# The first of sixteen rows: slot maxima ahead of the next row's statistics on VectorE, the second projection inside the expert product, one zero product moved

## The reference

```
xn  = layernorm(x)
out = x + attention(xn) + experts(xn)

attention: q,k,v = xn @ Wqkv + bqkv, 16 heads of 8; q and k normalised to length 1;
           feat = exp(clip(q_hat @ omega * sqrt(2 s) - s, -20, 20)) * const    (2 x 32 features)
           causal linear attention: ctx = (feat_q . feat_k, masked) @ v / denominator; @ Wout + bout
experts:   xn2 = rms_norm(xn) * gamma_x;  se = rms_norm(slot_embeds) * gamma_slot   (512 slots)
           logits = xn2 @ se.T                       (256 tokens x 512 slots)
           slots = softmax over tokens(logits).T @ xn2
           processed = gelu(slots @ w1) @ w2
           y = softmax over slots(logits) @ processed
```

## Time and profile before

| what | us |
|---|---|
| median of 3 runs | 448.09 |
| lowest, highest | 447.37, 450.14 |
| the profiled execution: its time | 448.38 |
| the profiled execution: its span | 446.6 |
| TensorE busy in the span | 434.6 (97%) |
| VectorE, ScalarE, GpSimd busy | 348.6, 320.1, 186.4 |

### The profile page before, as it was taken

The page is one execution under the profiler, slowest core; times in us unless marked ns, Lnnn a source line. Parts: engine busy times, 40 slices in busy tenths (PEclk is TensorE's granted clock), DMA queues, the critical chain, the costliest instruction groups (busy, mean ns, idle before and its releaser), DMA issues.

```text
span 446.6 us, 15786 instructions
## 1 busy us (share of the span) xinstructions
PE 434.6 (97%) x5726; PEld 363.9 (81%) x5726; DVE 348.6 (78%) x872; ACT 320.1 (72%) x533; POOL 186.4 (42%) x278
## 2 busy tenths in 40 slices
PE   6889999999999999999999999999999999999896
PEld 3578888898888889888888888888888888888785
DVE  7968796978778697877969787797978779676553
ACT  4648686867858687695868779586877858677681
POOL 5405564344345434444543444454344445434320
PEclk9889999999999999999999999999999999999999
DMA  4400302030200203020020302002020200303001
GB/s 93 105 25 2 61 12 52 14 60 16 47 26 9 50 12 59 12 47 24 5 54 12 58 12 47 24 2 57 12 57 14 47 12 1 60 1 61 2 1 25
DMA packets 45323, 14.37 MB, mean 32 GB/s; under 512 B 35376, under 2 KB 45168, under 8 KB 45296
## 3 DMA queue, kind: packets, MB, share of 16 engines
q1 hardware_dynamic: 44448, 13.48, 14.7%
q10 hardware_dynamic: 720, 0.53, 0.4%
q0 software_dynamic: 128, 0.01, 0.1%
HBM read 3.44 MB, written 2.10 MB: 12 GB/s over the span
## 4 chain that ended last, share of the span: by engine, by line
PE 93%; DVE 3%; ACT 2%; issue 1%; DVEq 0%; ACTq 0%
PE x L1070 19%; PE p_s L1120 10%; PE p_t L1120 8%; PE x L1238 8%; PE x L1271 7%; PE x L1280 6%; PE x L1292 6%; PE x L1133 5%; PE p_s L1133 5%; PE x L1211 3%; PE p_s L1105 2%; PE x L1222 2%; PE x L1246 2%; PE x L1187 2%; PE p_t L1105 1%; PE x L1230 1%
## 5 line engine op out<-in xcount | busy, mean ns | idle before, releaser
L488 POOL TENSOR_TENSOR s_sb<-s_sb,causal 128x256 f32<-128x256 f32 x96 | 68.4, 733 | 79.4 <-ACT s_sb L584 79.4
L578 ACT ACTIVATE feat<-arg,f_bias 128x1024 f32<-128x1024 f32 x64 | 71.7, 1147 | 8.4 <-DVE arg L848 8.3
L848 DVE TENSOR_SCALAR arg<-p_s,f_low,f_high 128x1024 f32<-128x1024 f32 x32 | 42.9, 1339 | 19.6 <-PE p_s L1105 13.1
L1120 PEld LDWEIGHTS p_s<-feat 64*64 64x64 f32 x1024 | 38.8, 132 | 17.1 <-issue 15.5
L329 POOL TENSOR_TENSOR qk_sq<-qkv 128x512 f32<-128x512 f32 x15 | 15.6, 1040 | 85.9 <-DVE qkv L825 85.9
L1120 PE MATMUL p_s<-feat 64*64 64x256 f32 (+3 forms) x1024 | 49.5, 309 | 1.3 <-ACT feat L578 1.3
L482 POOL TENSOR_TENSOR s_sb<-s_sb,causal 128x512 f32<-128x512 f32 x30 | 37.6, 1276 | 26.0 <-ACT s_sb L590 26.0
L1120 PE MATMUL p_t<-feat 64*64 64x256 f32 (+3 forms) x1024 | 47.1, 299 | 0.3 <-issue 0.3
L1120 PEld LDWEIGHTS p_t<-feat 64*64 64x64 f32 x1024 | 41.3, 133 | 1.8 <-issue 0.4
L848 DVE TENSOR_SCALAR arg<-p_t,f_low,f_high 128x1024 f32<-128x1024 f32 x32 | 42.7, 1334 | 0.0
L1238 PEld LDWEIGHTS x<-xg,disp 128*128 128x128 f32 x256 | 31.3, 199 | 8.2 <-ACT disp L606 8.2
(11 more groups left out here) (165 smaller groups left out, 1040.5 us busy)
## 6 DMA issues: line engine op xcount, KB each, us to landing
xin<-in_L_attn_x_dram SPq DMA_DIRECT2D x31, 64.0 KB, 2.3
out_dram<-out_sb SPq DMA_DIRECT2D x31, 64.0 KB, 2.1
se_rows<-n_L_ffn_slot_embeds_dram SPq DMA_DIRECT2D x2, 128.0 KB, 4.6
w_f<-in_L_ffn_w_dram SPq DMA_DIRECT2D x1, 256.0 KB, 4.1
w_sb<-in_L_ffn_w_dram SPq DMA_DIRECT2D x1, 256.0 KB, 4.0
stack_t<-stack SPq DMA_TRANSPOSE x16, 4.3
wqkv_f<-in_L_attn_Wqkv_dram ACTq DMA_DIRECT2D x1, 192.0 KB, 4.1
bqkv_bc<-in_L_attn_bqkv_dram ACTq DMA_DIRECT2D x1, 192.0 KB, 4.9
```

What stands on the lines that cost most here:

```text
L488: pool.tensor_tensor(v, v, m, ALU.mult).then_inc(mb_ok, 1)
L578: nc.scalar.activation(feat[:, k:k + 2, :], arg[:, k:k + 2, :], ACT.Exp, bias=f_bias[:, 0:1]).then_inc(fe_ok, 1)
L848: nc.vector.tensor_scalar(arg[:, k:k + 2, :], (p_s, p_t)[g % 2][:, :, :], f_low[:, 0:1], f_high[:, 0:1], ALU.max, ALU.min).then_inc(cl_ok, 1)
L1120: mm = nc.tensor.matmul(dst[rows:rows + 64, u, o:o + hi - lo], f[:, T + keys:T + keys + 64], f[:, lo:hi], start=True, stop=True, skip_grou ...
```

## The change

Row 0 alone is touched, and TensorE's start. Four edits:

1. VectorE: `slot_maxima(b)` and `ln_stats(b1)` go ahead of the three constants, `slot_maxima` first.
2. ScalarE: `ln_root(b1)` goes from ahead of `dispatch_exp` to between `dispatch_exp` and `combine_exp`.
3. TensorE: the second expert product's low part is issued as chunk 0, then `project` 2 and 3, then chunk 1.
4. TensorE: five zero products at the start instead of four, and one instead of two between `logits_turned` and `shift`.

```
@@ scalar
-            ln_root(b1)

             def first_row():

                 b, b2 = b0, step(b0, 2)
                 dispatch_exp(b)
+                ln_root(b1)
                 combine_exp(b)
@@ vector, first_row
                 token_maximum(b, 1)
+                slot_maxima(b)
+                ln_stats(b1)
                 dve.wait_ge(d_col, 32)
                 nc.vector.tensor_scalar(f_low[:, :], node_c[:, :], -CLIP, None, ALU.add)
                 nc.vector.tensor_scalar(f_high[:, :], node_c[:, :], CLIP, None, ALU.add)
                 dve.wait_ge(f_ln, 1)
                 nc.vector.tensor_tensor(f_bias[:, :], coef_ln[:, :], node_c[:, :], ALU.subtract).then_inc(f_ok, 1)
-                ln_stats(b1)
-                slot_maxima(b)
                 ln_newton(b1)
@@ tensor
-            def processed_low(b):
+            def processed_low(b, parts):
                 after(pe, ge_ok, count(b, 2, 1))
-                for m in (0, 1):
+                for m in parts:
...
-            zeros(4)
+            zeros(5)
             transposes(b0)
...
                 logits_turned(b)
-                zeros(2)
+                zeros(1)
                 shift(b)
...
-                processed_low(b)
+                processed_low(b, (0,))
                 project(b, 2)
                 project(b, 3)
+                processed_low(b, (1,))
                 processed_high(b)
...
-                processed_low(b)
+                processed_low(b, (0, 1))
```

## The result

| | before | changed |
|---|---|---|
| median of 6 runs each, us | 448.41 | 445.21 |
| lowest, highest | 447.37, 450.14 | 445.06, 445.88 |
| the profiled execution: time, span | 448.38, 446.6 | 445.07, 443.3 |
| mean granted clock of the profiled execution | 0.992 | 0.999 |

The ratio is 0.9927, 95% interval [0.9906, 0.9948]: 3.2 us faster. In what follows one execution of the kernel before, 484.63 us at a mean clock of 0.849, is left out as one of the chip's slow state.

What follows compares the result with a forecast made beforehand. TensorE was taken to bound rows 1 to 15, so only row 0's gain counts: -1.55 + 0.45 = -1.10 us gives 447.3 from the profiled execution, 447.0 from the median; forecast 447.1, range 445.8 to 448.9 (own range 446.4 to 447.8).

Steps and rivals of the forecast that it cites:

- The bound: Whole kernel: TensorE sets the time of rows 1 to 15, so row 0's gain or loss reaches the end unchanged.
- The new wait for `xg`: Row 0's slot sums: TensorE pauses up to 0.65 us for `xg` ahead of row 1's transposes.
- The second projection: Second expert product: first clip about 1 us earlier, next clip unmoved; costed at 0, ends 0.3 us gain or loss.
- The removed zero product: Ahead of row 0's shift: with one left, the removal costs nothing but a pause of 0.3 us.
- the term of the second low stretch: Row 0's transposes and slot sums: clock drops at 24.3 as before, 2.24 us stays, slot sums end 1.55 us earlier.
- gave 0.45 back: At `slots_transposed`: low clock still lasts, so it takes 1.12 us instead of 0.67, returning 0.45 of the gain.
- the sum: Whole change: -1.55 + 0.45 = -1.10 us, with the front zero product's delay already inside the -1.55.
- the rival with a kept clock: Row 0's slot sums: the clock does not fall, total gain 2.45 us, time 445.9 us; chance 0.17.
- the fifth zero product: TensorE's start: two more records delay row 0's transposes by 0.32 us, with 0 and 0.64 as ends.
- all of it arrives: Row 0's chain from transposes to logits has no slack, so `logits_turned` starts at 19.10 instead of 18.78.
- that hold under the exponentials: Row 1's statistics: `xres` may hold them until 22.4, still covered by ScalarE's exponentials; uncovered, up to 0.7 us reaches `xg`.
- a sign of being wrong: Row 1's root on ScalarE: the prediction is wrong if the statistics make ScalarE wait.

Runs made afterwards that it cites:

- filled pause: Kernel before, order untouched, with five zero products at the start and four instead of two ahead of the shift: median 447.48 us, ratio 0.9994.
- the version with later transposes: Changed kernel with row 1's transposes behind the second half of the slot sums, and slots_norm 1 ahead of xt_low: median 444.61 us, ratio 0.9927.

## Why the prediction was wrong

**Right.** The bound: row 0 alone decides, and what is gained at row 1's logits (3.32 us) is the difference of the spans (3.3). The maxima start 0.64 us behind the turned logits (forecast 0.69), take 1.29, and the shift follows at once. The new wait for `xg` is there (0.62 us, forecast up to 0.65). A statistics instruction is held by `xres` and mostly hidden by ScalarE (0.20 us is not, see below). The second projection moves one clip and nothing else. The removed zero product costs nothing.

**Wrong, first: the term of the second low stretch.** The prediction let the drop "come at the same time as before", kept 2.24 us for transposes and slot sums and gave 0.45 back at `slots_transposed`. In the changed kernel the same stretch, from 23.39 to 24.74, took 1.35 us at full clock, and `slots_transposed` 0.67. That is 0.89 and 0.45, or 1.3 us that the sum lacks. The pause ahead of the shift had shrunk from 1.43 to 0.30 us; the rival with a kept clock was this case, and its chance of 0.17 was far too low. Its own time, 445.9, is still 0.7 us above the measured one, since it too took the fifth zero product for a cost. The filled pause shows that the pause matters, and the runs with five zero products and the root behind the exponentials say how surely the clock stays up: 37 of 38 have one of 0.997 or more.

**Wrong, second: the zero products at the start.** I charged the fifth with 0.32 us for TensorE's start and gave it no effect. Executions differ in when the clock comes up: 7.3 us in the profiled one before, 5.8 in the one after, 4.5 to 7.1 in the others. Where it is up by 6.6 the delay is nil or under 0.1; at 7.12 it was the 0.32, and 0.76 at the turned logits, so "all of it arrives" was wrong too. That the profiled execution of the change paid nothing was luck of its clock. What it brings I had left out of the sum altogether: the first low stretch, 10.7 to 14.1, which goes with it. That was -0.72 us at the turned logits, where the sum had +0.32. That the product keeps this stretch away shows over many runs: in the new order 8 of 12 with four products have at least one low stretch, 1 of 38 with five. In the end it is worth less than the -0.72 suggests: with four, the fall that was traced cost 0.4 us at row 1.

**Put together.** From -1.10: +0.45 not given back and 0.89 in the slot sums make -2.44; -0.32 of delay that did not come makes -2.76; the first low stretch's 0.72 makes -3.48, of which the held L794 takes 0.20 back at the root and so at `xg`: 3.30 is what came. The prediction had that hold under the exponentials. But these came 1.08 us earlier than it forecast and `xres` only 0.60 (its end at 21.60, not 22.20), and so the cover was gone, by its own words a sign of being wrong. In causes that the filled pause separates, it is 1.86 by the clock and 1.44 by the order, between these two executions; half of the executions of the kernel before have at most one low stretch and lose less by the clock. The order gives 2.24 at the shift (22.28 against 20.04) and loses 0.80 of it again by the wait for `xg` and VectorE's scaling, which the version with later transposes recovers by 0.62.

**On the held instructions.** In the kernel before GpSimd's `omega_lo` held `f_bias` and then `w1_lo` held L793; in the changed kernel the reductions went through beside `w1_lo` (18.70 to 19.99, GpSimd's product from 19.66) in 1.29 us, as in row 1. The Trainium skill, "SBUF — State Buffer", section "Who interferes with whom", has it so: a VectorE instruction with two SBUF inputs, or a tensor_scalar in a two-port mode, and a reading GpSimd product exclude each other for the whole instruction, a tensor_reduce does not take part. The trace agrees, with 0.98, 1.16 and 0.77 us for instructions of 0.14 to 0.18, and no change for the reductions. Not every tiny instruction is held: `f_low` and `f_high`, 128x1 at 18.18 and 18.25, took 0.15 and 0.14 us in the kernel before, with `omega_lo` running from 18.11.

## What to carry to other kernels

A tiny instruction on VectorE can take as long as GpSimd's product beside it (0.17 us became 1.16): before one is put ahead of something that TensorE waits for, look at what GpSimd runs beside it, and put reductions from PSUM first. A pause of TensorE can cost twice, since the clock may fall in the products behind it (the slot sums took 1.90 us instead of 1.16); so a reordering that shortens a pause should be costed at both clock levels, and the low one kept only if a pause as long is still there. Read more than one execution's clock before a low stretch is taken as part of the kernel: the mean granted clock of each run sorts the kernel before into two groups, 1.65 us apart.

## What was not expected of the hardware

The clock came up at anything from 4.5 to 7.3 us after the start in the thirteen traces, with TensorE starting at 1.50 in all of them (told by the clock's first record and the spacing of the zero products), so one trace cannot say whether work near that time runs at 1.2 or 2.4 GHz. A transposing DMA that lands after 4.3 or 4.4 us took 6.2 once, and TensorE waited 1.44 us for it. One run in six has 0.6 to 1.3 us more around its span than the others, whatever the kernel.
